# Two moves by one step: the scan's delta on VectorE, and the expert scatters on GpSimd

## What is computed

```python
left  = silu(causal_dwconv(left))              # 128 inner channels
delta = softplus(u @ W_delta + b_delta)
h = exp(d_t * A) * h + (d_t * u_t) * b_t       # 64 states per channel, token after token
y = sum_n h_n * c_t_n
...
topk_w, topk_idx = top_k(softmax(x @ gate_w.T), cap)   # 16 experts, 512 tokens each, per sequence
eo   = (gelu(x_tok @ Wg) * (x_tok @ Wu)) @ Wd * topk_w
flat = zeros.at[topk_idx].add(eo)              # scatter-add into the tokens
x = x + s6_block * silu(flat + shared_expert)
```

## Time and profile before

| | us |
|---|---|
| median of 3 executions | 4805.53 |
| lowest, highest | 4796.07, 4806.9 |
| the profiled execution, its own time | 4796.07 |
| its span, first to last instruction | 4794.3 |

### The profile page before, as it was taken

The page is one execution under the profiler, slowest core; times in us unless marked ns, Lnnn a source line. Parts: engine busy times, 40 slices in busy tenths (PEclk is TensorE's granted clock), DMA queues, the critical chain, the costliest instruction groups (busy, mean ns, idle before and its releaser), DMA issues. The chain is left out here.

```text
span 4794.3 us, 68000 instructions
## 1 busy us (share of the span) xinstructions
PE 4093.5 (85%) x24660; PEld 3387.6 (71%) x24660; DVE 3474.5 (72%) x4975; ACT 2582.0 (54%) x4869; POOL 2586.9 (54%) x1858
## 2 busy tenths in 40 slices
PE   8899999979899999978888866767888888888864
PEld 7788888858788888857777755656676666667653
DVE  5466666655566666627888889988888788888887
ACT  6544444437344444447677653256666666666665
POOL 3122222233122210026666656878899889998987
PEclk9999999989999999989999967889999999999996
DMA  2022222221122210024444431255655556556658
GB/s 85 30 88 72 87 81 78 88 86 40 51 88 72 87 58 20 22 70 144 153 135 140 137 107 63 77 174 165 182 179 176 177 176 186 177 170 184 193 163 316
DMA packets 271490, 572.90 MB, mean 119 GB/s; under 512 B 37169, under 2 KB 157746, under 8 KB 271154
## 3 DMA queue, kind: packets, MB, share of 16 engines
q1 hardware_dynamic: 246578, 534.98, 33.4%
q0 software_dynamic: 24576, 33.57, 3.9%
HBM read 445.64 MB, written 122.81 MB: 119 GB/s over the span
## 5 line engine op out<-in xcount | busy, mean ns | idle before, releaser
L1536 POOL TENSOR_TENSOR scan_drive_sb<-scan_b_wide_sb,scan_du_sb 128x1024 f32<-128x1024 f32 x512 | 1301.1, 2562 | 317.5 <-DVE scan_h_sb L1448 310.6
L1448 DVE TENSOR_TENSOR_SCAN scan_h_sb<-decay_bank,scan_state_sb,scan_drive_sb 128x512 f32<-128x512 f32 x896 | 1116.7, 1268 | 99.7 <-ACT decay_bank L1786 96.2
L1786 ACT ACTIVATE decay_bank<-scan_delta_sb,a_neg_sb 128x512 f32<-128x512 f32 x1024 | 700.7, 687 | 375.0 <-DVE scan_h_sb L1448 370.5
L958 PE MATMUL ybank<-v_low_hi_lo_sb,pt_hi_b_sb 128*128 128x384 f32 x2048 | 663.5, 358 | 22.0 <-DVE pt_lo_b_sb L838 14.4
L1455 DVE TENSOR_TENSOR scan_ch_sb<-c_pair,scan_h_sb 128x1024 f32<-128x1024 f32 x512 | 614.3, 1200 | 69.6 <-PE c_pair L1623 68.1
L1634 PE MATMUL y_bank<-identity_sb,scan_ch_sb 128*128 128x128 f32 x4096 | 655.0, 293 | 5.0 <-ACT scan_temp_sb L1804 4.9
L838 DVE TENSOR_TENSOR pt_lo_b_sb<-pt,pt_hi_b_sb 128x512 fp32r<-128x512 f32 x512 | 353.0, 690 | 413.7 <-ACT pt_hi_b_sb L1001 413.7
L1634 PEld LDWEIGHTS y_bank<-identity_sb,scan_ch_sb 128*128 128x128 f32 x4096 | 549.9, 153 | 111.4 <-issue 15.2
L1623 PE MATMUL c_pair<-scan_cc_sb,select_state_sb 128*128 128x512 f32 x1024 | 386.2, 461 | 258.9 <-DVE scan_ch_sb L1455 257.9
L992 ACT ACTIVATE p_b_sb<-scores,softmax_cols_b_sb 128x1024 f32<-128x1024 f32 x256 | 285.8, 1116 | 552.0 <-DVE softmax_cols_b_sb L832 413.3
L959 PE MATMUL ybank<-v_low_hi_lo_sb,pt_lo_b_sb 128*128 128x256 f32 x2048 | 572.3, 279 | 0.0
(11 more groups left out here) (325 smaller groups left out, 9912.0 us busy)
## 6 DMA issues: line engine op xcount, KB each, us to landing
scan_b_wide_sb<-b_scratch SPq DMA_DIRECT2D x512, 512.0 KB
w_hi_scratch<-split_hi_sb SPq DMA_DIRECT2D x51, 512.0 KB, 2.8
w_lo_scratch<-split_lo_sb SPq DMA_DIRECT2D x51, 512.0 KB, 4.1
expert_hi_sb<-w_hi_scratch SPq DMA_DIRECT2D x48, 512.0 KB
expert_lo_sb<-w_lo_scratch SPq DMA_DIRECT2D x48, 512.0 KB
x_b_sb<-x SPq DMA_DIRECT2D x16, 512.0 KB, 4.0
g_scratch<-g_out_b_sb SPq DMA_DIRECT2D x16, 512.0 KB, 3.0
split_raw_sb<-WgT SPq DMA_DIRECT2D x16, 512.0 KB, 5.5
```

The source lines that it names most:

```text
L958: e.matmul(k.y_bank[:, 0:D + P], k.pt_hi[n % 2][:, cols], kv.v[:, block, :], start=(kb == 0), stop=False, skip_group_check=True)
L1448: e.tensor_tensor_scan(k.h[i % H_BUFFERS][:, j, :], k.decay_banks[S % DECAY_BANKS][:, :], k.drive[i % DRIVE_BUFFERS][:, j, :], start, ALU. ...
L1536: e.tensor_tensor(k.drive[i % DRIVE_BUFFERS][:, :, :], k.b_wide[i % B_BUFFERS][:, :, :], k.du[c % 2][:, :].unsqueeze(1).broadcast_to([P, P ...
L1786: e.activation(k.decay_banks[S % DECAY_BANKS][:, :], k.delta[c % 2][:, :], ACT.Exp, scale=wt.a[:, n:n + 1]).then_inc(k.s_decay, 1)
```

## The change

DVE's `delta(c)` moves from step `DELTA_AT + 8` = 32 of the preparation to step 31. POOL's `scatter` moves from three steps behind its down product to two. Nothing else differs: no instruction, no buffer, no semaphore.

```diff
@@ scan_vector, prepare
-            if s == DELTA_AT + 8:
+            if s == DELTA_AT + 7:
                 delta(c)
@@ moe_gpsimd, routed
     def routed(q, s):
-        h, j = part(UP_AT, s - 3), part(DOWN_AT, s - 3)
+        h, j = part(UP_AT, s - 3), part(DOWN_AT, s - 2)
         if s < SLOT_TILES:
             gather(q - ALL_GROUPS, s)
```

## The result

The changed kernel takes 4830.84 us (median of 5 executions, 4827.26 to 4832.94) against 4804.31 us before (5 executions, 4796.07 to 4806.9). It is slower by 0.54%: the ratio is 1.0054, with a 95% interval of 1.0042 to 1.0065. All thirteen executions of it on record lie between 4818.37 and 4832.94 us, with a median of 4830.79. The forecast was 4811 us with a range up to 4828, and "same" was the likeliest case, at 0.67. So the time lies outside the range, by 3 us, and "slower", which was given 0.22, came true.

A forecast was written before the change was run, and what follows sets the result against it. DVE, with what ACT and PE hand it, was taken to set the pace, POOL having some 6 us to spare. 8 + 0.5 - 2.6 = +5.9 us on 4796.07 gave 4802, forecast median 4811 us, range 4796 to 4828.

The forecast's parts named there:

- same: Whole kernel: no change told from 0.3%, so neither below 4791 nor above 4820 us; chance 0.67.
- slower: Whole kernel: above 4820 us, from most of the POOL rival and part of the DVE rival; chance 0.22.
- I take half, 8 us: DVE, delta one step earlier: between 0 and 15.5 us of delay, half stays on the path, 8 us.
- 0.5 us: POOL's earlier scatters: one passed drive, around 3516 us, is delayed beyond its margin, 1.8 against 1.3 us; cost 0.5 us.
- Edit 1, the mechanism: DVE: moved delta still starts when POOL's softplus ends; its wait grows and the passed scan comes 1.2 us later.
- Delta passes exactly one scan: DVE's order in a pair: delta at step 31 goes ahead of one scan, 1.2 us, in 15 counted cases.
- DVE keeps the whole delay: Rival: all 15.5 us of delta's delay stay on DVE, +13.4 us, 4819 us; chance 0.17.
- five waits of 1.3 to 6.2 us: DVE within 15 us behind delta: waits for ACT's copy of C or PE in five of 15 cases, absorbing delay.
- Edit 2, the drives: POOL: drives delayed by waiting scatters, up to 2.4 us, stay hidden by their 6 to 8 us of margin.
- POOL is the bound after all: Rival: delays of the scatters add to the end, 12 + 8 - 2.6 = +17.4 us, 4823 us; chance 0.14.
- I count all 2.6: End of the scan: last scatter passes one drive, goes 2.6 us earlier, and the last stage's loads with it.
- the upper bounds of 15.5 and 12 us: Most that delta's delays on DVE (15.5 us) and the scatters' delays on POOL (12 us) could add.

The follow-up runs named there:

- b1: The kernel before, unchanged, timed against itself: ratio 1.0002.
- b2: The kernel before, unchanged, timed against itself once more: ratio 1.0007.
- e7: Changed kernel with scatters two steps behind only in blocks 9, 19 and 26, three in the other 29: 1.0052 against before, +24.2 us.
- The second timing: The changed kernel, both edits, timed again beside its two halves on one chip: 1.0047 against before, +22.3 us.
- e8: Kernel before with delta at step 33 and POOL's product delta * u at step 34 instead of 33, scatter as before: 0.9994, -4.5 us.

## Why the prediction was wrong

Three terms of the sum 8 + 0.5 - 2.6 failed. "I take half, 8 us" measured 11 and 13 us by the timings, and 18 to 20 us in the stretches; "0.5 us" for the scatters left out the softplus, for 8 us in the stretches; and the end gave 1 to 2 us, not 2.6. Another 10 us or so, in the timings only, were in no term, and their cause stays open.

**Edit 1, the mechanism: right; its upper bound low.** Delta passed a scan, started when POOL's softplus ended, and the wait fell on DVE. 15.5 us were counted as the most it could add; the stretches around the deltas grew by 18 and 20 us (from 313.0). "Delta passes exactly one scan" is the step that was short: in five chunks it passes work of the experts on DVE, too, and the stretches of four of these grow by 1.7 to 2.9 us instead of 1.2. Delta itself takes 26.3 us in the fifteen chunks instead of 24.4. Most of that is in the chunk near 2270 us, which was forecast to gain 0.6 us: delta took 0.67 us alone there and takes 2.83 us beside a drive, behind a wait of 1.1 us. That chunk's stretch is too unsteady to show what it cost.

**Edit 1, "I take half, 8 us": mis-sized.** It measured 11 and 13 us in the timings. By these a third comes back and not half, of 19 and not of 15.5; in the traces hardly any does (first to last scan +21 and +16 us). So the rival "DVE keeps the whole delay", with 15.5 us for this part and a chance of 0.17, was nearer than the prediction's own 8 us: a little by the timings (12 us), clearly by the traces. The prediction took five waits of 1.3 to 6.2 us behind delta for waits on somebody else's work. Of these the waits for ACT's copy of C were as long in the changed kernel (15.0 us against 13.6); my reading, not tested by itself, is that PE and ACT reach that work through instructions that wait for DVE, and so arrive as much later as DVE does. What shrank is the wait for ACT's decays, from 120.7 and 122 us to 115 to 117 with delta alone, and to 110.6 with both edits.

**Edit 2, the drives: right.** POOL's wait for the weighings was forecast at 35 to 40 us; it came out higher, at 50.0 us in the whole kernel with delta moved, and 44.0 and 45.1 with the scatter alone. POOL's wait for scans was to fall: over the earlier trace rows's stretch of the work it does with the scatter alone (42.8 and 37.5 us against 43.4 and, in b1 and b2, 43.3 and 47.2), and rises with delta moved, where the scans come later. No drive was late for its scan. The rival "POOL is the bound after all" is refuted by that, though its time, 4823 us, came closest.

**Edit 2, "0.5 us": the second term that failed.** The softplus was named among what is queued behind a late scatter, and then only the drives were weighed. A drive has 6 us of margin, the softplus has none, since DVE already stands waiting for it in 13 of 16 chunks. In two chunks a scatter moved ahead of it, and in a third POOL reached it 1.8 us late behind a longer wait for a weighing, for 8 us in the stretches; e7 shows that these three blocks alone do that.

**The end, "I count all 2.6": somewhat too much.** The chain of the changed kernel and the wait of ACT for the last load, for the earlier trace rows, and POOL's last scatters:

```profile
4691.47 3.71 DMA moe_scratch<-moe_out_sb,moe_rows_sb
4696.07 5.38 DMA final_s_sb<-s_scratch
```

```profile
4701.48 1.06 ACT L2690 ACTIVATE final_m_sb<-final_m_sb 128x1024 f32<-128x1024 f32 x1 [5.73 <-DMA final_s_sb<-s_scratch]
```

```profile
4684.50 1.58 POOL L2278 DMA_INDIRECT moe_scratch<-moe_out_sb,moe_rows_sb  x1 [0.58 <-ACT moe_out_sb L2182]
...
4689.60 1.56 POOL L2278 DMA_INDIRECT moe_scratch<-moe_out_sb,moe_rows_sb  x1 [1.10 <-ACT moe_out_sb L2182]
4691.47 1.57 POOL L2278 DMA_INDIRECT moe_scratch<-moe_out_sb,moe_rows_sb  x1 [0.30 <-ACT moe_out_sb L2182]
```

ACT's wait fell from 8.80 to 5.73 us. But the last three scatters now wait for their weighings (0.58, 1.10, 0.30 us), which come when PE has the down products ready. From scan 950 (counted from 0) to the last scan it is 147.2 and 147.6 us with both edits against 148.1 to 148.6 in the three traces of before, 1 us less; to the end of the span it is 195.3 and 194.5 against 196.6 to 196.9, some 2 us less. The traces of the other kernels reach 199.7 us there, so this is no sharp number.

**The sum.** Forecast 8 + 0.5 - 2.6 = 5.9 us; measured 26.5 and 22.3 us. Of the difference the timings give 4 us to delta (12 for 8) and 3 to the scatter alone (0 to 3 us where -2 were forecast). The other 10 or 11 us appear only where both edits are in. In the stretches the two add, 19 and 8 us apart and 27 together, so there the scatter's part is no larger with delta moved than without. Set against the timings, of the single edits 7 and some 6 us come back elsewhere, and of both together only 3. DVE's other waits don't bear this out: they fall by 4 and 9 us with both edits, and by 1 and 6 us with delta alone. Whether the same idle time can't be used twice, or the scatters take it away, no run here decides: of the kernels with delta ahead, the one without any moved scatter costs 11 to 13 us, and those with all, with three blocks and with the other 29 all cost 22 to 26. So the timings say that the parts do not add, by 10 us with an uncertainty of 6, while the traces from first to last scan show them adding; which holds, and why, is open.

**The range** was too narrow above because it ended at the upper bounds of 15.5 and 12 us less the gain of the end, 4830, cut to 4828, and the change reached that sum. The second timing, 22.3 us above before, stays under the 24.9 us of the two upper bounds; the first, 26.5 us, does not.

## What to carry to other kernels

Before moving an instruction ahead on the engine that sets the pace, look whether it already waits: if it does, every step ahead puts other work of that engine behind the wait, and the step back is the one to try. In this kernel it was worth 0.23%. For a moved instruction on an engine with slack, don't ask only for the margin of its bulk work; find the one consumer with no margin and see whether the moved work passes in front of it. When you count what a moved instruction passes, count every generator that writes into that engine's stream. And before you let a wait further down absorb a delay, ask whether the one it waits for itself depends on the delayed engine; that this is why so little was absorbed here is my reading and was not tested.

## What the runs showed of the hardware

Delta reads two tiles in SBUF (both inputs of its `scalar_tensor_tensor` are `k.temp` tiles), and its duration depends on what POOL does beside it: 0.69 us next to an indirect DMA, 1.73 to 1.77 us next to a subtraction of 128x512 that starts with it and takes 1.3 us, 2.81 us next to a drive of 2.34 us, and 5.18 us in e8, next to two drives in a row. In each of these but the first it ends 0.55 us past the end of POOL's instruction. The Trainium skill, SBUF — State Buffer, Who interferes with whom, says that a VectorE instruction with two SBUF inputs contends with a GpSimd instruction that reads SBUF; the traces agree, and show that the lost time stands in the instruction's duration and not in the idle time before it, so that a list of waits misses it.

An indirect DMA that scatters 128 rows takes 1.54 to 2.08 us of POOL (median of 128 in the trace of before: 1.59), and two in a row start 1.9 us apart (3675.75 and 3677.65). For comparison, the softplus's L1504, 128x512, takes 1.28 us. So it has to be counted when the order of POOL's stream is laid out.
